# Computing most of the experts' blocks inside layer 2's slots instead of after them

## The reference

```python
def _gcn_layer(x, W, b, src, dst, norm, n_nodes):
    xt = x @ W
    msg = xt[src] * norm[:, None]
    agg = jax.ops.segment_sum(msg, dst, num_segments=n_nodes)
    return jax.nn.relu(agg + b)
norm = edge_weight * jax.lax.rsqrt(deg_out[src] * deg_in[dst] + EPS)
h7 = _gcn_layer(_gcn_layer(_layernorm(x), W6, b6, ...), W7, b7, ...)
x = x + (h7 @ Wp + bp)
# experts, on the layer norm of x: 8 of them, each token goes to its top 2
for e in range(8):
    h = gelu(xn @ W1[e] + b1[e])            # 256 -> 512
    y = y + (h @ W2[e] + b2[e]) * w_full[..., e, None]   # 512 -> 256
x = x + y
```

## Time and profile before

| | |
|---|---|
| median of 3 runs | 3762.37 us (3759.31 to 3781.63) |
| the profiled execution | 3770.5 us, its span 3768.7 us |
| busy, share of the span | PE 79%, DVE 53%, POOL 53%, ACT 37% |
| chain that ended last, by engine | PE 32%, POOL 17%, DVE 16%, DMA 14%, issue 13% |

### The profile page before, as it was taken

One profiled execution on the slowest core, in us unless ns is written; L12 is line 12 of the kernel. 1 busy time (PEld: TensorE's weight loads), 2 busy tenths in 40 slices (PEclk: granted clock), 3 DMA queues, 4 the chain that ended last, 5 costly groups with the idle time before them and its releaser, 6 DMA issues.

```text
span 3768.7 us, 58473 instructions
## 1 busy us (share of the span) xinstructions
PE 2971.0 (79%) x17257; PEld 2012.5 (53%) x17257; DVE 1995.7 (53%) x7494; ACT 1383.2 (37%) x3657; POOL 1990.0 (53%) x2006
## 2 busy tenths in 40 slices
PE   4577289999999999996678888888888664588885
PEld 3456145555555555554445555555555422477774
DVE  7999876777777677761202333343333354433332
ACT  5577355555555555541301111111111110344552
POOL 0000177556655565566367777777777773133332
PEclk9989699999999999998989988999998765799998
DMA  3001355555455555547546766666666643233334
GB/s 102 0 18 36 90 166 160 163 162 157 133 161 160 159 163 163 154 139 252 150 142 191 233 206 202 201 202 202 194 202 202 220 128 80 56 58 58 59 59 104
DMA packets 208606, 535.62 MB, mean 142 GB/s; under 512 B 42925, under 2 KB 138437, under 8 KB 202053
## 3 DMA queue, kind: packets, MB, share of 16 engines
q0 software_dynamic: 105936, 263.26, 28.2%
q1 hardware_dynamic: 99796, 253.82, 19.1%
q10 hardware_dynamic: 2592, 15.16, 1.0%
HBM read 380.42 MB, written 158.05 MB: 143 GB/s over the span
## 4 chain that ended last, share of the span: by engine, by line
PE 32%; POOL 17%; DVE 16%; DMA 14%; issue 13%; ACT 5%; DVEq 2%; SPq 1%; ACTq 0%; POOLq 0%
POOL arena L798 15%; PE bank L1716 11%; DMA acc<-arena 7%; PE bank L1708 7%; DVE arena L935 3%; DMA zrow<-zsum 3%; ACT arena L1445 3%; PE bank L1730 2%; DMA sorted_x<-arena 2%; PE bank L1740 2%; PE bank L1742 2%; PE bank L1857 2%; DVE arena L1105 2%; PE bank L1867 2%; PE bank L1762 1%
## 5 line engine op out<-in xcount | busy, mean ns | idle before, releaser
L798 POOL DMA_INDIRECT arena<-table,src_i x1792 | 1718.3, 959 | 852.1 <-issue 514.5
L1716 PE MATMUL bank<-arena 128*128 128x257 f32 x4704 | 1218.2, 395 | 5.8 <-ACT zcd L1462 5.8
L1716 PEld LDWEIGHTS bank<-arena 128*128 128x128 f32 x4704 | 876.2, 196 | 237.9 <-issue 116.0
L1453 ACT ACTIVATE arena<-arena 128x128 bf16<-128x128 bf16 x1440 | 487.2, 393 | 324.7 <-DVE arena L1087 319.6
L1708 PE MATMUL bank<-arena 128*128 128x343 bf16 x2160 | 459.2, 324 | 174.4 <-ACT arena L1453 93.0
L1105 DVE TENSOR_TENSOR arena<-arena,bank 128x343 f32 x720 | 366.2, 509 | 362.5 <-PE bank L1708 271.4
L1708 PEld LDWEIGHTS bank<-arena 128*128 128x128 bf16 x2160 | 188.0, 99 | 416.6 <-DVE arena L1105 172.1
L1730 PE MATMUL bank<-arena,s_all 128*32 128x257 f32 x3584 | 281.6, 438 | 144.6 <-DMA arena<-table,src_i 129.7
L845 POOL DMA_INDIRECT acc<-arena x105 | 168.3, 1603 | 343.5 <-ACT arena L1561 238.5
L1436 ACT COPY zs<-bank 128x257 f32<-128x257 f32 x224 | 83.2, 371 | 554.8 <-PE bank L1730 540.3
L1680 PE MATMUL bank<-arena 128*128 128x150 bf16 x1616 | 188.0, 275 | 113.5 <-DVE arena L935 111.9
(11 more groups left out here) (216 smaller groups left out, 3391.9 us busy)
## 6 DMA issues: line engine op xcount, KB each, us to landing
chunks<-arena SPq DMA_DIRECT2D x24, 3307.5 KB
arena<-chunks SPq DMA_DIRECT2D x22, 3307.5 KB, 13.6
arena<-table,src_i POOLq DMA_INDIRECT x1792
zsum<-zc SPq DMA_DIRECT2D x224, 64.2 KB
arena<-sorted_x SPq DMA_DIRECT2D x105, 132.5 KB, 2.1
zrow<-zsum SPq DMA_DIRECT2D x50, 257.0 KB, 4.2
arena<-in_W ACTq DMA_DIRECT2D x16, 512.0 KB, 15.3
arena<-chunks ACTq DMA_DIRECT2D x2, 3307.5 KB, 17.3
```

Of the source, the lines that this page charges most:

```text
L798: pool.indirect_dma_start(gat[:, r, j, :], None, table[L], bass.IndirectOffsetOnAxis(ap=src_i[:, col:col + 1], axis=0)).then_inc(gathered[ ...
L1453: last = act.activation(parts[:, r, i], ohl[:, r], ACT.Copy, scale=w3f[:, i, t:t + 1])
L1716: last = pe.matmul(ps_ap, adj[:, c % 2, h, 0:P], xp[:, h], start=(h == 0), stop=(h == XB_ALL - 1))
```

## The change

Layer 2's slots become 129 (n = 0 to 128). After each pair's places are known, DVE lists the blocks of 128 rows that are certain to be full by then (`list_pair`, four a pair, 90 in all, by the counts of tokens so far). These 90 blocks are computed inside the slots 31, 35 to 42, 44 to 79, 81 to 84 and 88 to 128, one a slot, at the earliest `BLOCK_LAG` = 8 slots behind the pair's last stage (4 for the last pairs). The other 15 are listed and computed at the end, as all were before. Which expert a block belongs to is known only at run time, so SP reads the expert and the first row from the list into registers and loads that expert's W1 (two DMAs), b1 and W2 (four DMAs) for each block from HBM, with the block's rows. The first 61 blocks have one set of tiles, the later ones two. The tiles take the place of arrays that are no longer read; s_mat has 2 buffers instead of 4, zrow and zr one instead of two in layer 2. DVE's copies of the weights and ACT's load of all weights are gone.

POOL's turn n now holds the sends of the pair that began at slot n-7 or n-8, two a turn, one before and one after the turn's gathers, and then the add of the block of slot n-4. Because sends write `sorted_x` and block loads read it, the code fixes their order on both sides: `sends_before_block` and `blocks_before_send`. Adds and the pairs' stores, which both write `acc`, are ordered the same way.

In layer 1 the 49 products of a chunk are spread over 26 steps instead of 25, and a chunk's buffer is cleared in four slices (16, 16, 13 and 4 column blocks) behind steps 8, 16, 23 and 25, in place of two (26 and 23).

```diff
 CAP = 6400
 PAY = 265
-XB_RING = 3
 BLOCKS = 105
-SEND_LAG = 7
+S_RING = 2
+Y_RING, ROW_RING, LIST_RING = 3, 4, 4
+POOL_LEAD = 4
+BLOCK_LAG, LATE_LAG, LATE_FROM = 8, 4, 108
 PARTS_OUT = 16

 TINY_EW = 2.0 ** -15
...
             return 2 * it - 1 + u // CT, u % CT - STEP_FROM

-        STEPS = ceil_div(XB_ALL, 2)
-        HALF_STEP = 12
-        HALF_HI = 2 * (HALF_STEP + 1)
+
+        STEPS = CT - 4
+        ZERO_BEHIND = (8, 16, 23, STEPS - 1)
+        SLICES = len(ZERO_BEHIND)
+
+        def first_of_step(step):
+            return XB_ALL * step // STEPS
+
+        def slice_bounds(i):
+            return first_of_step(ZERO_BEHIND[i - 1] + 1) if i else 0, first_of_step(ZERO_BEHIND[i] + 1)

...
+        def whole_blocks(i):
+
+            tokens = min(i * PT * P, N)
+            return max(0, ceil_div(2 * tokens - NE * (P - 1), P))
+
+
+        LISTED = [range(whole_blocks(i), whole_blocks(i + 1)) for i in range(NPAIR)]
+        STREAMED = whole_blocks(NPAIR)
+
+        def block_slots():
+            at, slot = [], 0
+            for i, (start, b) in enumerate(STARTS):
+                for _ in LISTED[i]:
+                    last = start + PAIR_SLOTS - 1
+                    slot = max(slot + 1, last + (BLOCK_LAG if last < LATE_FROM - PAIR_SLOTS else LATE_LAG))
+                    at.append(slot)
...
+
+        BLOCK_SLOT = block_slots()
+        BLOCK_AT = {slot: j for j, slot in enumerate(BLOCK_SLOT)}
+        PAIR_OF = [i for i in range(NPAIR) for _ in LISTED[i]]
+        SLOTS = max(BLOCK_SLOT[-1], STARTS[-1][0] + PAIR_SLOTS - 1) + 1
+        TWO_SETS = sum(slot <= 4 * CHUNKS + 3 for slot in BLOCK_SLOT)
...
+        def set_of(j):
+
+            return 0 if j < TWO_SETS else (j - TWO_SETS + 1) % 2
+
+        def uses_before(j):
+            if j < TWO_SETS:
+                return j
+            return (TWO_SETS if set_of(j) == 0 else 0) + (j - TWO_SETS) // 2
+
+        def blocks_before(j):
+
+            if j < TWO_SETS:
+                return j
+            return 0 if j == TWO_SETS else j - 1
+
+
+        SENDS = {(i, q): start + PAIR_SLOTS - 1 + POOL_LEAD + q // 2 for i, (start, b) in enumerate(STARTS)
+                 for q in range(2 * PT)}
+        ADDS = [slot + POOL_LEAD for slot in BLOCK_SLOT]
+
+        def sends_before_block(j):
+
+            least = 2 * PT * (PAIR_OF[j] + 1)
+            return max(least, sum(at <= BLOCK_SLOT[j] for at in SENDS.values()))
+
+        def blocks_before_send(k):
+            return sum(sends_before_block(j) <= k for j in range(STREAMED))
+
+        def adds_before_store(i):
+            return sum(at <= STARTS[i][0] + PAIR_SLOTS for at in ADDS)
+
+        def stores_before_add(j):
...
-            def store_acc(i, b):
+            def store_acc(i, b, adds):
                 sp.wait_ge(acc_ready, i + 1)
+                if adds:
+                    sp.wait_ge(y_added, 16 * adds)
                 sp.dma_start(pair_rows(acc, b), xs).then_inc(acc_stored, 16)
...
+            def load_up(j, e, first):
+                s, n = set_of(j), blocks_before(j)
+                if n:
+                    sp.wait_ge(h_mm, n)
+                    sp.wait_ge(gelu_done, n)
+                for k in range(KD):
+                    sp.dma_start(w1_e[s][k], A["W1"][:, bass.ds(e * (KD * H) + k * H, H)]).then_inc(w1_in[s], 16)
+                sp.dma_start(b1_e[:, s], A["b1"][:, bass.ds(e * HC, HC)]).then_inc(w1_in[s], 16)
+                if n:
+                    sp.wait_ge(xe_T, n)
+                    sp.wait_ge(cols_made, n)
+                sp.dma_start(xe[s], sorted_x[bass.ds(first, P), :]).then_inc(xe_in[s], 16)
+
+            def load_down(j, e):
+                s, n = set_of(j), blocks_before(j)
+                if n:
+                    sp.wait_ge(y_mm, n)
+                for c in range(HC):
+                    sp.dma_start(w2_e[s][c], A["W2"][:, bass.ds(e * (HC * D) + c * D, D)]).then_inc(w2_in[s], 16)
...
-                def layer2_slot(n, c, j, g, stage):
+                def layer2_slot(n, c, j, g, stage, blk):
+                    if blk is not None:
+                        load_down(blk, experts.pop(blk))
                     if stage and stage[2] == 0:
...
@@ -716,8 +837,17 @@
                         merge_rows(1)
                         store_rows(1, CHUNKS - 1)
                     if stage and stage[2] == PAIR_SLOTS - 1:
-                        store_acc(stage[0], stage[1])
-
+                        store_acc(stage[0], stage[1], adds_before_store(stage[0]))
+                    then = BLOCK_AT.get(n + 1)
+                    if then is not None:
+                        i = PAIR_OF[then]
+                        sp.wait_ge(listed, 1 + sum(len(js) > 0 for js in LISTED[:i]))
+                        e, first = listed_block(list_i[:, i % LIST_RING], first_i[:, i % LIST_RING], then - LISTED[i][0])
+                        sp.wait_ge(sent, 16 * sends_before_block(then))
+                        load_up(then, e, first)
+                        experts[then] = e
...
+                for s in range(2):
+                    reads = sum(set_of(j) == s for j in range(reads_before(i, q)))
+                    if reads:
+                        pool.wait_ge(xe_in[s], 16 * reads)
                 pool.indirect_dma_start(sorted_x, bass.IndirectOffsetOnAxis(
                     ap=idx_i[:, slot, q // 2, q % 2:q % 2 + 1], axis=0), zx[:, slot, q // 2, :], None).then_inc(sent, 16)
+
+            def reads_before(i, q):
+                return blocks_before_send(2 * PT * i + q) if isinstance(i, int) else 0
+
+            def add_block(j):
+
+                pool.wait_ge(y_ready, j + 1)
+                if j:
+                    pool.wait_ge(y_added, 16 * j)
+                pool.indirect_dma_start(acc, bass.IndirectOffsetOnAxis(ap=row_e[:, j % ROW_RING:j % ROW_RING + 1], axis=0),
+                                        ye[j % Y_RING], None, compute_op=ALU.add).then_inc(y_added, 16)

...
+                    for i, q in some[:1]:
+                        send(i, i % 2, q)
                     if n < L1_GROUPS:
                         gathers(1, n)
-                    turn = STAGE_AT.get(n - SEND_LAG)
-                    if turn:
-                        i, _, q = turn
+                    for i, q in some[1:]:
                         send(i, i % 2, q)
+                    for j in range(STREAMED):
+                        if ADDS[j] == n:
+                            pool.wait_ge(acc_stored, 16 * max(stores_before_add(j), PAIR_OF[j] + 1))
+                            add_block(j)
             with pool.Else():
                 for L in range(2):
                     pool.wait_ge(do_in_table, 16 * (L + 1))
...
+            def list_last():
+
+                n = BLOCKS - STREAMED
                 dve.tensor_copy(fill_i, next_of[:, :])
...
-            def block_weights(j, e):
-
-                if j > 1:
-                    dve.wait_ge(h_mm, j - 1)
-                dve.tensor_copy(w1_e[:, j % 2].rearrange("p k h -> p (k h)"),
-                                w1_sb[:, bass.ds(e, 1)].rearrange("p a n -> p (a n)")).then_inc(w1_made, 1)
-                if j > 1:
-                    dve.wait_ge(gelu_done, j - 1)
-                dve.tensor_copy(b1_e[:, j % 2], b1c[:, bass.ds(e * HC, HC)]).then_inc(b1_made, 1)
...
+                ends = Links(dve, last_links)
+                row = list_blocks(ends, many, n, n, last_f[:, 0:n], last_i[:, 0:n], lastfirst_i[:, 0:n], last_row[:, 0:n],
+                                  False)
+                none = many.rows[:, 0:n, 0]
+                ends(dve.tensor_scalar(none, last_f[:, 0:n], float(NE), float(FILL), ALU.is_ge, ALU.mult))
+                dve.tensor_tensor(lastfirst_i[:, 0:n], row, none, ALU.max).then_inc(counted, 1)
...
+            def block_cols(j, expert):
+
+                s, n = set_of(j), blocks_before(j)
+                pick.at(j)
+                dve.wait_ge(cols_made, j)
+                dve.wait_ge(xe_in[s], uses_before(j) * 16 + 16)
+                pick(dve.scalar_tensor_tensor(out=picked, in0=iota_f[:, 0:NE], scalar=expert, in1=xe[s][:, D:D + NE],
+                                              op0=ALU.is_equal, op1=ALU.mult), wait_apart)
+                if n:
+                    dve.wait_ge(y_ready, n)
+                dve.tensor_reduce(w_e[:, s:s + 1], picked, AX_X, ALU.add)
+                if j >= ROW_RING:
+                    dve.wait_ge(y_added, (j - ROW_RING + 1) * 16)
+                dve.tensor_copy(row_e[:, j % ROW_RING:j % ROW_RING + 1], xe[s][:, PAY - 1:PAY]).then_inc(cols_made, 1)
...
                     copy_chunk(1, n // 4 - 1)
-                if n == 4 * CHUNKS:
-                    load_experts()
                 if g is not None:
                     copy_sums(1, g)
+                if blk is not None:
+                    block_T(blk)
                 if stage:
                     stage_of(stage[0], stage[2])
                 if g is not None:
                     copy_rows(1, g)
```

(17 more changed lines are left out.)

379 lines of the change are left out of this document (216 added, 163 removed).

## The result

The changed kernel took **4062.4 us** (median of 4 runs, 4056.6 to 4064.4), the kernel before 3766.6 beside it: **1.078 times as long (95% interval 1.076 to 1.080)**. The forecast was 3899 in a range of 3660 to 4080. The direction came as forecast, and so did the ring between sends and loads (a ring is a closed circle of waits, each engine waiting for the next). The forecast size, 3.6%, was less than half of the 7.8% measured, and one term of the sum carries most of that. The 4062 lies inside the range only because the range reached into case 3; it is just above the forecast's own case (3790 to 4060).

A forecast was written before the change was run, and what follows sets the result against it. POOL was taken to bound layer 2 before the change. Last blocks -409, layer 1 -40, slots 31 to 111 +476, slots 112 to 128 +125, gap -15 gave +137 us: 3907, or 3899 as median, range 3660 to 4080.

The forecast's parts named there:

- the ring between sends and loads: Layer 2 slots: sends and block loads wait for each other, gathers between two sends; 20.6 or 23.4 us between blocks' rows.
- case 3: Rival for the whole kernel, slow PE and crowded DMA: turns at 24 and 28 us, other slots 17; 4210 us, chance 0.12.
- the forecast's own case: Whole kernel: the summed forecast of 3899 us, with 3790 to 4060 as its span; chance 0.58.
- I take 6 us (ends 4.9 and 8): Last 15 blocks: 6 us each from bytes loaded and SP's issues, 90 us in place of 499, so -409.
- -40 (ends 0 and -58): Layer 1: clearing a chunk in four pieces shortens DVE's 22 waits for ACT by 2 us each; 40 us less.
- Slots 31 to 111, +476: Layer 2 slots taking most moved blocks: 1391 us against 915 before, 476 us more.
- both kinds of turn: Layer 2 turns with sends: 20.6 us for the first kind, 23.4 for the second, where SP stands at the pair's store.
- Slots 112 to 128 with the gap: End of layer 2: 17 slots at 12.1 us, +125, and a shorter gap before the last blocks, -15.
- Slots 0 to 31: Layer 2 from slot 0 to slot 31: forecast difference 0.
- The first (the ring does not bind): Rival: sends and loads pass each other early, block slots take PE's 14.5 us; 3588 us, chance 0.10.
- the second (its low ends): Rival: turns with sends at 18.5 us, other block slots at 14, about even or faster; 3688 us, chance 0.20.

The follow-up runs named there:

- e2: Changed kernel, but in the last 15 blocks SP issues the next block's first weights and rows ahead of this block's second weights: 4720 us, ratio 1.100, slower chips.
- e7: Changed kernel, but SP issues a block's rows ahead of its first weights: 4655 us, 1.085 times the kernel before, slower chips.
- e8: Changed kernel with the four orders of e1, e2, e6 and e7 together: 4564 us, 1.063 times the kernel before, slower chips.
- e10: e9 with the edits of e2 and e7 added: 4037 us, 1.069 times the kernel before, faster chips.
- e14: e13 with the edits of e1, e2 and e7 added: 3837 us, 1.017 times the kernel before, faster chips.
- e3: Changed kernel, but each weight DMA moves an eighth of its bytes, all waits and products kept: 4704 us, 1.095 times the kernel before, slower chips.
- e4: Kernel before with the change's layer 1 part alone, no block moved: 0.9987 times the kernel before (0.9966 to 1.0009), slower chips.
- e1: Changed kernel, but a turn's eight gathers are issued ahead of both its sends, not between them: 4607 us, 1.072 times the kernel before, slower chips.
- e6: Changed kernel, but a pair's store waits only for adds of earlier turns, not the same turn's: 4707 us, 1.095 times the kernel before, slower chips.
- e17: e14, but SP issues the next block's loads ahead of the chunk load and the pair's store: 4357 us, 1.016 times the kernel before, slower chips.
- e9: Changed kernel, but the fixed order between sends and block loads is set two slots looser: 4229 us, 1.119 times the kernel before, faster chips.
- e13: e9 with the order of stores and adds loosened as well: 4128 us, 1.094 times the kernel before, faster chips.
- e16: e11 with the order of stores and adds alone loosened by one slot: 4010 us, 1.063 times the kernel before, faster chips.
- e11: Changed kernel with the edits of e1, e2 and e7, without the store's: 3861 us, 1.021 times the kernel before, faster chips.
- e18: e11, but SP issues the next block's loads ahead of the chunk load and store: 4510 us, 1.053 times the kernel before, slower chips.
- e5: The changed kernel again, unedited, for comparison on the slower chips: 4773 us, 1.110 times the kernel before.
- e12: The kernel before, run again for its trace, on the faster chips: slot 0 at 1901.9 us, slots 31 to 111 in 913.0.

## Why the prediction was half right

**The step that failed: "I take 6 us (ends 4.9 and 8)" for the last blocks.** I priced a block by what has to be moved (bytes, SP's eight issues) and never walked the waits in the order in which SP and PE stand. The runs showed in its place a ring (SP's loads wait for PE's second product, PE's transposes for the rows behind those loads) of 13.6 us a block, beyond my upper end. That is 108 of the 149 us by which the sum was off. Shown by e2 (next block first: 10.1), e7 (rows first: 12.0), e8, e10 and e14 (both: 6.0 to 6.5) and by e3 (an eighth of the bytes: nothing). That 6 fits a program which the change did not contain is luck: it came from the bytes.

**Layer 1, "-40 (ends 0 and -58)".** -18 in this pair of traces, about -9 over all of them, and 15 at most by e4. That is 22 of the 149. (22 waits at 2 us are 44, not 40.) 46.4 of the 57.6 us of waiting are left, and the trace of the changed kernel says why (clearings L1639, tile operations L1647):
```profile
757.42 1.66 ACT L1639 COPY arena<-zero 128x1755 f32<-128x1755 f32 x1
758.98 1.27 ACT L1647 ACTIVATE arena<-arena 128x128 bf16<-128x128 bf16 x4
760.16 0.62 ACT L1639 COPY arena<-zero 128x540 f32<-128x540 f32 x1
```
The last clearing does take 0.62 us in place of 2.8, but on ACT it stands behind the third one and four tile operations. DVE begins to wait at 759.15, 1.0 us before it begins; at the next chunk it is 1.7 us.

**Slots 31 to 111, +476: right**, at +503, as were both kinds of turn (20.1 and 24.9 for 20.6 and 23.4) and the order of the four slots. e1 shows that the gathers between the sends are in it, e3 that the weights' bytes hardly are, e6 that the store is in the second kind. (In the earlier trace rows the 4.26 us stand behind 4.95 us of idle time; the 5.72 that the prediction puts there come later.) Slots 112 to 128 with the gap: +91 for +110. Slots 0 to 31, costed at nothing: +11, with no single cause shown.

**The rivals.** The first (the ring does not bind) fell with the waits and e1, the second (its low ends) with 20.1 and 24.9 us. The third, slow PE and crowded DMA, fell with e3, as far as the weights crowd, and with clocks of 0.91 and 0.85 in the two stretches. Where PE did run slow, in the first products of the last blocks, it was behind 8 us of idle time. That a chunk load's traffic delays an add behind it, and with it the store and the next rows, I had only as an end of the second kind's range; in e14 it seems to be what was left, though e17, which takes the rows out from behind it, keeps a slot of 28 us.

**Where the gain went.** The end is 301 us shorter. The slots that took the blocks over are 605 us longer (11 + 503 + 91): 90 blocks at 4.75 us were sold for 90 slots that grew by 6.7 us each. PE's part of a block fits into 11.5 and 13.8 us in two slots of four in e14; what made the others long were the orders on POOL and SP. That other orders would make the move pay is not shown, since none tried did.

## What to carry to other kernels

When two engines' DMAs on one tensor are ordered one by one, write down all that lies between two successive ones; a wider distance between the partners changes nothing of it and can put more in between (e9 and e13 were slower than the changed kernel, e16 slower than e11). It paid in one pair of runs, 153 us from e18 to e17, where the ring was already short. Price a loop of few stages by walking every queue in its program order, not by bytes: blocks of 6 us were 13.6 because of the order of three loads. When several edits each shorten a ring, run them together before adding them: -404 in parts was -209 in one.

## What was not expected of the hardware

Three chips took 4287 to 4292 us for the kernel before, the first chip and two others 3767 to 3776. Instructions last the same (DVE's add to a chunk 0.51 us on both, a gather 0.96 and 0.95), and so do the last blocks (13.6 us). The difference is in stretches where engines work hand in hand: a tile of chunk building takes 2.06 us instead of 1.69 in the changed kernel (e5 and the first trace). DVE's waits before its adds, from 500 to 1600 us, of the kernel before on A (e12):
```profile
DVE arena L1105 <- issue: 25.4, 14, 3.2
```
and with e4's edits on B:
```profile
DVE arena L1111 <- remote: 136.3, 36, 20.6
DVE arena L1111 <- issue: 74.8, 50, 2.8
```
Both names stand for idle time whose releaser the profile doesn't show. The clock granted is not it (0.97 in both traces from 1000 to 1300 us, where the building is 20% slower). Its cause stays open. It is why an effect should be measured beside both kernels on one chip: 7.8% on A was 11.0% on B.
